# Projection pieces between the two score pairs of a chunk, and the first shift rows loaded earlier, in a decoder layer on Trainium2

## The reference

```python
def _L0_xattn_ref(x, context, Wq, bq, Wk, bk, Wv, bv, Wo, bo):   # x (8,512,256), context (8,1601,256)
    q = x @ Wq.T + bq            # 16 heads of 16
    k = context @ Wk.T + bk
    v = context @ Wv.T + bv
    scores = jnp.einsum('bhtd,bhcd->bhtc', q, k) / jnp.sqrt(d)
    attn = jax.nn.softmax(scores, axis=-1)
    out = jnp.einsum('bhtc,bhcd->bhtd', attn, v)
    return out @ Wo.T + bo
x = x + _L0_attn_ref(_layernorm(x), ...)
x = x + _L0_xattn_ref(_layernorm(x), ctx_1024, ...)
x = x + _L0_ffn_ref(_layernorm(x), ...)
```

## Time and profile before

| | |
|---|---|
| time before, median of 3 runs | 2397.34 us (2396.11 to 2414.44) |
| the profiled execution's own time | 2399.05 us |
| its span, first to last instruction | 2396.9 us |
| instructions | 35042 |
| busy: PE / DVE / ACT / POOL | 91% / 63% / 48% / 18% |
| mean granted TensorE clock | 0.954 |
| stages in the span | retention to about 348 us, prologue 348 to 464, chunks 464 to about 1960, feed-forward to the end |

### The profile page before, as it was taken

How to read it: one execution, slowest core, us unless ns; L and a number is a source line. 1 busy time by engine, 2 the same in 40 slices (tenths; PEclk the granted TensorE clock), 3 DMA queues, 4 the chain that set the end, 5 groups by cost and what they waited for, 6 DMA issues and landing times. The chain is left out here.

```text
span 2396.9 us, 35042 instructions
## 1 busy us (share of the span) xinstructions
PE 2174.8 (91%) x12914; PEld 1201.8 (50%) x12946; DVE 1511.4 (63%) x2944; ACT 1158.0 (48%) x1521; POOL 431.2 (18%) x470
## 2 busy tenths in 40 slices
PE   6888867599999999999999999999999978899999
PEld 4656544244444444444444434444443337778887
DVE  6888874476676676676667677667668827622221
ACT  2313121156666666666656666666666663222222
POOL 1101021002102112112111210210211005332222
PEclk9999986589999999999989999999999998999999
DMA  4000005504223321520630531422341001000000
GB/s 160 1 0 0 0 4 100 110 1 100 56 56 82 74 56 50 106 56 2 141 69 1 100 95 16 100 55 56 74 81 29 1 16 59 0 9 9 18 18 18
DMA packets 45360, 118.58 MB, mean 49 GB/s; under 512 B 9120, under 2 KB 21408, under 8 KB 45088
## 3 DMA queue, kind: packets, MB, share of 16 engines
q1 hardware_dynamic: 45232, 116.88, 21.9%
HBM read 77.30 MB, written 38.81 MB: 48 GB/s over the span
## 5 line engine op out<-in xcount | busy, mean ns | idle before, releaser
L1142 DVE TENSOR_REDUCE x_mx<-x_ps 128x1 f32<-128x512 f32 x1536 | 956.1, 684 | 400.8 <-PE x_ps L897 400.1
L1050 ACT ACTIVATE x_probs<-x_ps 128x1024 f32<-128x1024 f32 (+1 forms) x832 | 810.2, 1021 | 507.9 <-PE x_ps L956 507.9
L897 PE MATMUL x_ps<-x_kst,x_qst 48*128 48x512 f32 x1536 | 591.4, 467 | 67.9 <-issue 23.9
L897 PEld LDWEIGHTS x_ps<-x_kst,x_qst 48*128 48x128 f32 x1536 | 264.7, 192 | 583.9 <-DVE x_mx L1142 446.4
L956 PE MATMUL x_ps<-x_qst,x_kst 50*128 50x512 f32 (+1 forms) x1664 | 498.3, 432 | 2.5 <-ACT x_probs L1050 2.4
L944 PE MATMUL x_ps<-x_probs,x_vst 128*17 128x512 f32 (+1 forms) x3328 | 449.1, 612 | 6.3 <-ACT x_ou L1034 5.9
L956 PEld LDWEIGHTS x_ps<-x_qst,x_kst 50*128 50x128 f32 (+1 forms) x1664 | 259.3, 185 | 66.4 <-ACT x_probs L1050 49.9
L1569 DVE TENSOR_TENSOR f_hid_whole<-f_ps,f_act_g 128x512 f32<-128x512 f32 x80 | 55.2, 691 | 241.5 <-PE f_ps L1326 232.9
L1441 ACT ACTIVATE f_act_g<-f_ps 128x512 f32<-128x512 f32 x80 | 47.7, 596 | 246.3 <-remote 126.4
L1507 POOL TENSOR_TENSOR f_hid_rest<-f_hid_whole,f_hid_rounded 128x512 fp32r<-128x512 f32 x80 | 103.1, 1289 | 234.0 <-ACT f_hid_rounded L1447 234.0
L1082 POOL TENSOR_TENSOR x_vst<-x_v_all,x_bv 128x768 f32<-128x768 f32 x64 | 66.4, 1069 | 428.0 <-ACT x_v_all L1009 349.4
(11 more groups left out here) (191 smaller groups left out, 2540.6 us busy)
## 6 DMA issues: line engine op xcount, KB each, us to landing
x_kst<-k_parts SPq DMA_DIRECT2D x192, 200.1 KB, 8.6
k_parts<-x_kp SPq DMA_DIRECT2D x16, 1601.0 KB, 6.1
x_ctxT<-in_ctxT SPq DMA_DIRECT2D x8, 1601.0 KB, 7.4
x_qst<-q_parts SPq DMA_DIRECT2D x192, 64.0 KB, 2.4
q_parts<-x_qp SPq DMA_DIRECT2D x8, 1024.0 KB, 4.3
x_all<-in_x SPq DMA_DIRECT2D x8, 512.0 KB, 3.8
out<-x_all SPq DMA_DIRECT2D x8, 512.0 KB, 2.9
x_qst<-x_mrows SPq DMA_DIRECT2D x128, 4.0 KB
```

Source lines behind the costliest of these rows:

```text
L897: m = pe.matmul(o, qst[mg][rows, pair, t * P:(t + 1) * P], kst[mg][rows, pair, i * 512:(i + 1) * 512], start=True, stop=True)
L1050: nc.scalar.activation(probs[0:w, s % 4, :, :], ps[0:w, 2 * (s % 2):2 * (s % 2) + 2, :], ACT.Exp, scale=HD ** -0.5).then_inc(exp_done, 1)
L1142: nc.vector.tensor_reduce(out=mx[:, 2 * pair + half, t, i:i + 1], in_=o, axis=AX.X, op=ALU.max).then_inc(drained_v, 1)
```

## The change

Within a chunk the piece comes between the score pairs: first list with pair 0, piece, second list with pair 1, values. PE, ACT (which now drains the piece between the two exps) and the order of STREAM follow, and with it DVE and the rotation of the banks. In the prologue the splits of the second half of k go from DVE to POOL, between `place_v(0)` and `place_v(1)`, and SP sends the shift rows of group 0 ahead of the loads of groups 2 and 3.

```diff
@@ work_of
-    return [[(first[g][c], second[g][c], pieces[g][c]) for c in range(SC)] for g in range(G)]
+    return [[(first[g][c], pieces[g][c], second[g][c]) for c in range(SC)] for g in range(G)]
@@ sync
             spill_q(0)
-            for f in range(KT):
-                spill_k(0, f)
-                load_group(0, 2 * f)
-                load_group(0, 2 * f + 1)
+            spill_k(0, 0)
+            load_group(0, 0)
+            load_group(0, 1)
+            spill_k(0, 1)
             load_shift(0, done(LEADER, ("shift", 0)))
+            load_group(0, 2)
+            load_group(0, 3)
@@ tensor
+            def woven(b, g, c, pair, n, some):
+
+                ahead = len(some) - 1 if some and all(item[0] == "max" for item in some) else 0
+                for i in range(ahead):
+                    fill(b, n + i, g)
+                scores(b, g, c, pair)
+                for i in range(ahead, len(some)):
+                    fill(b, n + i, g)
+                return n + len(some)
+
@@ tensor, the loop over chunks
-                        *woven, pieces = PLANS[b][g][c]
-                        for pair in range(2):
-                            some = woven[pair]
-                            ahead = len(some) - 1 if some and all(item[0] == "max" for item in some) else 0
-                            for i in range(ahead):
-                                fill(b, n + i, g)
-                            scores(b, g, c, pair)
-                            for i in range(ahead, len(some)):
-                                fill(b, n + i, g)
-                            n += len(some)
+                        first, pieces, second = PLANS[b][g][c]
+                        n = woven(b, g, c, 0, n, first)
                         for i in range(len(pieces)):
                             fill(b, n + i, g)
-                        n += len(pieces)
+                        n = woven(b, g, c, 1, n + len(pieces), second)
                         if c:
                             values(b, g, c - 1)
@@ scalar, the loop over chunks
-                        for item in [item for part in PLANS[b][g][c] for item in part]:
-                            if item[0] in BY_ACT:
-                                drain(b, n, g)
-                            n += 1
+                            for item in [item for part in PLANS[b][g][c][2 * pair:2 * pair + 2] for item in part]:
+                                if item[0] in BY_ACT:
+                                    drain(b, n, g)
+                                n += 1
@@ gpsimd
-            for g in range(G):
+            place_v(0)
+            for item in k_pieces(1):
+                split_k(pool, nc.gpsimd, 0, item[1], item[2], done(LEADER, item))
+            for g in range(1, G):
                 place_v(g)
@@ vector
-                elif item[0] == "k":
+                elif item[0] == "k" and item[1] == 0:
                     split_k(dve, nc.vector, 0, item[1], item[2], NTH[n])
```

## The result

The changed kernel takes 2259.66 us, median of 4 runs (2255.78 to 2262.7), against 2405.89 for the kernel before, also the median of 4: a ratio of 0.939, 95% interval 0.933 to 0.945. The forecast was 2243, range 2199 to 2291, counted from 2397.34: a gain of 154, where 146 were measured by the two medians. The profiled execution took 2255.78 us with a span of 2254.0, 142.9 less than before.

The account below looks back on a forecast made before the run. The prediction took the order of PE and DVE, neither engine itself, to bound the kernel. Chunks save 129 and the prologue 25.5: 2399.05 - 129 - 25.5 = 2244.5, so 2243 us against the median 2397.34; range 2199 to 2291.

Parts of the forecast that it names:

- What bounds the chunk: Chunk stage: neither PE nor DVE is the bound but their order; PE waits for DVE twice per chunk with a piece.
- The new chunk: Full-piece chunk with the piece between the score pairs: 3.40 us instead of 3.93, saving 0.53, bounds 0.23 to 0.73.
- The 0.1 into the piece: Chunk, from the first slot's end to the piece: changing the array from two halves to all rows costs 0.1 us.
- The norm chunks: The 30 chunks beginning with a score pair and tails: 3.39 us to an estimated 3.04, 10 us in all.
- The rule that spoke against the change: Chunk: a tiling mode change drains PE, with four changes instead of three; a full drain puts the saving at the low bound.
- Part one: All chunks with the new order: 115 + 10 + 7 - 3 = 129 us saved, bounds 50 to 175.
- Part two: Prologue: DVE without its splits and shift rows sent earlier; PE starts at 438.6, 25.5 us earlier.
- the 2.4: End of prologue: the shift sends land about 2.4 us later, from the median of the 64 KB loads.
- The context: First group, v piece of chunk 6: context lands about 465, wanted at 469, or at 461 with high clock, waiting 4 us.
- A wait for the context in the first group: Sign of being wrong: PE waiting for the context transfer in the first group's chunks.
- The sign that did not show as said: Sign of being right: PE's maxima weight loads nearly stop waiting for DVE's reduce, 431.7 us in 643 waits before.
- The rival of the early clock: Prologue and first chunks: less idle time makes PE's clock rise early, giving 2232 us; chance 0.15.

Follow-up runs that it names:

- the short reduces: Kernel before and changed kernel, each with DVE's maxima reduces over 64 instead of 512 columns: 2161.04 and 2162.22 us, one run each.
- `after_again`: The changed kernel unaltered, timed again on one chip with other versions: 0.9395 of the kernel before, median 2259.19 us.
- `short_reduce_before`: Kernel before with each reduce of maxima over 64 instead of 512 columns: 2161.04 us, one run; full-piece chunk 3.28 instead of 3.93.
- `prologue_only`: Kernel before with only the prologue's changes (SP's order, splits on POOL), chunk order as before: 0.9909 of the kernel before.
- `late_v`: Changed kernel with the seven v pieces of group 3 moved to chunks 1, 4, 6, 8, 9, 11 and 12: 2259.73 us, one run.
- `evac_early`: Changed kernel with the evacuation in chunk 1 of a group ahead of that chunk's first exp: 0.9285 of the kernel before, median 2232.39 us.
- `evac_context`: Changed kernel with both the early evacuation and the context loaded ahead of groups 2 and 3: 0.9250 of the kernel before, median 2226.95 us.
- `piece_front`: Changed kernel with the piece ahead of both score pairs instead of between them: 2358.23 us, one run.
- `pool_splits_only`: Kernel before with only the splits of the second half of k moved to POOL, SP's queue as before: 2402.2 us, one run.
- `context_first`: Changed kernel with the second sequence's context loaded ahead of groups 2 and 3: 0.9357 of the kernel before, median 2251.19 us.
- `shift_first_only`: Kernel before with only the shift rows sent ahead of the loads of groups 2 and 3, DVE splits kept: 2384.74 us, one run.
- `mid_only`: Kernel before with only the new chunk order, piece between the score pairs, prologue as before: 0.9478 of the kernel before.

## Why the prediction was right, and by how much it was off

- *What bounds the chunk*: right, and shown by the short reduces. PE lost 0.65 us a full-piece chunk to DVE: 0.47 by the fourth max (1.29 against 0.82) and 0.64 by the piece (1.88 against 1.24). The busy share of PE hid it.
- *The new chunk*: 3.37 for 3.40, short ones 3.28 for 3.29, shift chunks 3.29 for 3.29. The 0.1 into the piece and the 0.31 from the fourth max to values were 0.09 and 0.32. The wo chunks fell from 4.78 and 4.84 to 4.24 and 4.36. The norm chunks gained less than forecast: 0.24 each (3.61 to 3.37 from exp to exp), not 0.35.
- *The rule that spoke against the change*. The array's change, with the further start, costs 0.09 us here. The Trainium skill, TensorEngine Tiling (Array Packing), Key Properties, says that a change of mode drains the engine; the experiment agrees that it costs something, and puts it far below the 0.26 that the prediction estimated for a full drain.
- *Part one*, forecast 129. A sequence with high clock fell from 190.1 to 171.8, six times 110; groups 1 to 3 of the first from 143.6 to 128.2, 15; the last one by about 1.5: 127.
- *Part two*, forecast 25.5, measured 23.8, or 24.6 without the later start of the prologue. The shift was on ACT at 436.6, not at 433.8: the prologue began 0.8 late, and a turn was 5.5, not 5.2, as six reduces take 3.68 and not 3.6, and DVE idled 1.8 us and not 1.6, with 1.0 of reduces left at the piece's start where I took 1.2. The sends landed faster than I took: scores started 1.2 us behind the last send, not 2.4. That made up for 1.2 of the 2.8 us and was luck: the 2.4 was borrowed from loads of 64 KB.
- *The context*: the term that failed. I had it land at 465 and PE come at 469 or, with the clock up, at 461 and wait 4 us at most. The clock did rise early, at 450, PE came at 465.6 and the transfer at 469.5: it was sent at 450.7, not 448, and took longer. The step named the wait rightly, but I took the case without it; the low stretch from 467 to 487 behind it I had not priced. The first group took 58.5 us instead of 56.0, where I had reckoned with no loss. In `after_again` it took 55.9 with a wait of 0.72 us, so the 2.5 belong to this execution as much as to the kernel. A wait for the context in the first group stood among my signs of being wrong; it came, and the early high clock ahead of it made up for most of it.
- *What was not in the sum*: falls of the clock in later sequences, 4 us more than before in this execution, most in the last sequence, and 1 us more after the chunks. 23.8 + 127 - 2.5 - 5.4 = 142.9, the difference of the spans. By the medians the gain is 146 against 154 forecast. The forecast lies 17 us under the 2259.66 measured; half of that is the kernel before, whose median came out at 2405.89 and not at 2397.34.
- *The sign that did not show as said*: the waits of L899 for DVE were to be nearly gone, and 162.1 us remain in the view. The chunks with a full piece lost them; the view's sum was a poor sign, as said above. The range has a small slip too: its upper end is counted from 2399.05 and its lower one from 2397.34.
- *The rival of the early clock* came true in its condition and was worth nothing, since the context and the second low stretch took it back.

## What to carry to other kernels

Where two engines hand a small ring of buffers around and neither is full, look at the order in which work meets the ring: a burst longer than the ring makes the producer wait, and the consumer then idles behind it. Put the work that needs nothing of that consumer into the middle of the burst, and pay the price of one more change. After such a gain read again which small transfer is sent behind large ones, and which wait stands on a drain that could go ahead of longer work: here both together were worth another 1.5% (0.9395 to 0.9250), in part through the clock. Before summing up waits by what the view names, look whether the engine was idle or busy with other work during them.

## What the runs showed of the hardware

- One further change from two half-array matmuls side by side to a matmul over all rows and back, with the further start of a run, costs 0.09 us at the high clock (3.37 against 3.28, `short_reduce_before` and the changed order).
- Four sends of 4 KB behind 24 loads of 64 and 200 KB let PE start 11.8 us after the last send was issued (452.32 to 464.09); ahead of the loads it was 1.2 us (439.07 to 440.28).
- The clock rises at very different times after the chunks begin. From the first scores to the rise it took 9.5 to 10.3 us in the changed kernel's two executions, `prologue_only`, `late_v`, `evac_early`, `evac_context` and `piece_front`, 15 in `pool_splits_only`, but 26 in the kernel before, `context_first` and `shift_first_only` and 31 in `mid_only`, with PE busy throughout (9.00 of 9.00 us in the row from 441, 25.00 of 25.00 in the earlier trace rows). The order of the transfers does not decide it: `context_first` (26) and `evac_context` (10) have the same one.
- A wait of 0.56 us in a chunk that is otherwise dense can stand at the start of 7 to 17 us at 1.2 GHz, which cost 3 to 6 us in the sequences 1 to 6. Without the wait falls were rarer (4 of 12 sequences instead of 21 of 30), with more matmuls ahead of it they were not (4 of 6), and with short reduces and a wait of 1.02 us there was none (0 of 12). What sets them off stays open.
